# Attention and routed convolution on one core: memory tokens by a factor, the lower part of x formed earlier, lower filters last

## The reference, cut to what matters

```
xn  = rmsnorm(gn(x)) * g1                       # gn: 32 groups of 4 channels
q,k,v = w_qkv @ xn                               # 4 heads of 32 channels
k = concat([mem_k, k], tokens); v = concat([mem_v, v], tokens)   # 4 memory tokens
q = softmax(q, channels of a head) * DHEAD**-0.5
k = softmax(k, tokens)                           # over the 4 + 1024 tokens
context = k @ v.T ;  out = context.T @ q         # per head
x = x + rmsnorm(w_out @ out + b_out) * g2
# second block: 3x3 convolution whose filters are a sum of 3 experts, weighted
# per image and input channel by gates from a small routing network on pooled gn(x)
x = x + conv(gn(x), sum_k r[k] * expert[k])
```

## Time and profile before

| what | value |
|---|---|
| median of 3 runs | 440.47 us (439.46 to 441.87) |
| span of the profiled execution | 438.3 us |
| PE busy | 414.9 us, 95% |
| VectorE busy | 351.1 us, 80% |
| ScalarE busy | 296.2 us, 68% |
| GpSimd busy | 265.0 us, 60% |
| granted TensorE clock | 90% or more of full speed in each of 40 slices |

### The profile page before, as it was taken

The page is one execution under the profiler, slowest core; times in us unless marked ns, Lnnn a source line. Parts: engine busy times, 40 slices in busy tenths (PEclk is TensorE's granted clock), DMA queues, the critical chain, the costliest instruction groups (busy, mean ns, idle before and its releaser), DMA issues.

```text
span 438.3 us, 8984 instructions
## 1 busy us (share of the span) xinstructions
PE 414.9 (95%) x2651; PEld 367.2 (84%) x2651; DVE 351.1 (80%) x769; ACT 296.2 (68%) x908; POOL 265.0 (60%) x249
## 2 busy tenths in 40 slices
PE   7789898999999999999999999999999999999987
PEld 6688787979898988889797988888898989778777
DVE  3565989797989889797989798898989696987540
ACT  2785857868676858778676868688686868654131
POOL 4754739567583939486674939385874748252330
PEclk9999999999999999999999999999999999999999
DMA  7420242216252442506262433516162523424331
GB/s 195 178 98 2 96 193 98 120 72 241 99 218 119 146 192 95 229 28 228 98 241 96 175 160 126 208 53 230 52 239 96 192 97 114 175 98 191 146 143 48
DMA packets 19075, 61.63 MB, mean 141 GB/s; under 512 B 3024, under 2 KB 4320, under 8 KB 19040
## 3 DMA queue, kind: packets, MB, share of 16 engines
q1 hardware_dynamic: 19040, 61.21, 37.0%
HBM read 19.29 MB, written 8.39 MB: 63 GB/s over the span
## 4 chain that ended last, share of the span: by engine, by line
PE 43%; DVE 22%; issue 17%; ACT 11%; DMA 2%; POOL 1%; DVEq 0%; SPq 0%; ACTq 0%; POOLq 0%
PE ps_conv L1282 13%; PE ps_y L1214 6%; PE ps_att L1181 5%; DVE w_full L1020 5%; ACT expert_raw L662 4%; DVE y_scaled L908 3%; DVE route_terms L974 3%; ACT qk L601 3%; PE ps_y L1204 3%; PE ps_y L1220 3%; DVE q_exp L860 2%; DMA xa<-in_x_dram 2%; ACT squares L574 2%; PE ps_qkv L1160 2%; PE ps_qkv L1162 2%
## 5 line engine op out<-in xcount | busy, mean ns | idle before, releaser
L601 ACT ACTIVATE qk<-ps_qkv,scale 128x256 f32<-128x256 f32 x128 | 55.7, 471 | 5.9 <-PE ps_qkv L1162 3.5
L544 POOL TENSOR_TENSOR left_hi<-zeros 128x32 fp32r<-128x32 f32 x16 | 9.4, 585 | 78.9 <-DMA right_lo<-img_lo 78.9
L668 ACT ACTIVATE w_hi<-w_full 128x1152 fp32r<-128x1152 f32 x16 | 18.7, 1168 | 52.9 <-DVE w_full L1026 52.9
L537 POOL TENSOR_TENSOR w_lo<-w_full,w_hi 128x1152 fp32r<-128x1152 f32 x16 | 42.8, 2675 | 11.0 <-ACT w_hi L668 6.1
L492 POOL TENSOR_TENSOR x_lo<-x,x_hi 128x1024 fp32r<-128x1024 f32 x16 | 38.4, 2399 | 13.1 <-ACT x_hi L591 13.1
L518 POOL TENSOR_TENSOR scale<-ssq,minus_half 128x8 f32<-128x8 f32 x16 | 26.2, 1639 | 32.9 <-DVE ssq L901 32.9
L642 ACT ACTIVATE y_scaled<-ps_y 128x128 f32<-128x128 f32 x128 | 33.5, 294 | 14.5 <-PE ps_y L1214 14.5
L1160 PE MATMUL ps_qkv<-wqk_hi,x_hi 128*128 128x256 f32 x128 | 40.6, 317 | 2.5 <-ACT x_nt L582 1.3
L1282 PE MATMUL ps_conv<-left_lo,w_hi 128*128 128x512 f32 (+2 forms) x96 | 40.6, 424 | 0.0
L1282 PE MATMUL ps_conv<-img_hi,w_hi 128*128 128x512 f32 (+1 forms) x96 | 36.4, 393 | 2.5 <-issue 1.4
L1282 PE MATMUL ps_conv<-right_hi,w_hi 128*128 128x512 f32 (+2 forms) x96 | 37.9, 395 | 0.0
(11 more groups left out here) (172 smaller groups left out, 1337.5 us busy)
## 6 DMA issues: line engine op xcount, KB each, us to landing
xa<-in_x_dram SPq DMA_DIRECT2D x16, 512.0 KB, 4.1
xb<-in_x_dram SPq DMA_DIRECT2D x16, 512.0 KB, 4.7
left_hi<-img_hi SPq DMA_DIRECT2D x16, 511.5 KB, 2.9
right_hi<-img_hi SPq DMA_DIRECT2D x16, 511.5 KB, 3.7
left_lo<-img_lo SPq DMA_DIRECT2D x16, 511.5 KB, 2.9
right_lo<-img_lo SPq DMA_DIRECT2D x16, 511.5 KB, 3.7
out_dram<-expert_raw SPq DMA_DIRECT2D x15, 512.0 KB, 2.9
expert_raw<-_conv_expert_weight_dram SPq DMA_DIRECT2D x1, 1728.0 KB, 9.0
```

Of the source, the lines that this page charges most:

```text
L537: nc.gpsimd.tensor_tensor(w_lo[p][:, :, :].rearrange("p t o -> p (t o)"), w_full[:, :], w_hi[p][:, :, :].bitcast(F32).rearrange("p t o -> ...
L601: nc.scalar.activation(qk[:, t, :], ps_qkv[t % 2][:, 0:QK], ACT.Copy, scale=scale1[:, t:t + 1]).then_inc(qkv_done, 1)
```

## The change

- Memory tokens: their share of the softmax differs from one image to the next only by one factor per channel, exp(memk_max - k_max_all). Their exponents, their product with the values and with w_out are formed once (`memory_weights`, `memory_keys`, `memory_context`, `memory_mix`). Per image ACT forms `mem_factor` and the denominator `k_den`, VectorE `mem_scale` and `mix_base`, and `mix_evacuate` adds `mix_base` in place of the bias. The two PE products with the memory tokens and the small subtraction and exponent are gone.
- `k_shift` is a transpose in place of a product.
- `high1` on ACT stands before the results and the upper filters; `low1` on POOL stands before `image_edges`, and `x_scale` behind `normalise1`.
- In a convolution the products with the lower filters come last, so that only these wait for w_lo.
- `spreads` has two operations for both columns, a square and a sum, in place of one operation for each column.
- `gn2_mean` is on ACT; two convolution products stand before `y_transpose` in place of after it.

```diff
@@ POOL
             def step(t, p):
                 do(rms1, t, p, 3)
                 do(routing_products, t, p, 5)
-                do(x_scale, t, p, 3)
                 turn(inverse_deviations, t, p, 2)
                 do(gn1_shift, t, p, 2)
                 do(normalise1, t, p, 2)
+                do(x_scale, t, p, 3)
                 do(rms2, t, p, 4)
+                do(low1, t, p, 2)
                 do(image_edges, t, p, 5)
                 do(filters_low, t, p, 5)
-                do(low1, t, p, 2)
                 do(q_normalise, t, p, 3)
@@ ACT
+            def memory_factor(b, p):
+                nc.scalar.activation(mem_factor[:, :], k_max_all[:, :], ACT.Exp, bias=memk_max[:, :], scale=-1.0).then_inc(mem_factor_done, 1)
+            def k_denominator(b, p):
+                nc.scalar.activation(k_den[:, :], mem_sum[:, :], ACT.Identity, bias=k_x[:, C:C + 1], scale=mem_factor[:, :]).then_inc(k_den_done, 1)
...
                 do(qkv_evacuate, t, p, 2, 7)
+                do(high1, t, p, 1)
                 do(results, t, p, 5, 0)
                 do(filters_high, t, p, 4)
                 do(q_exponent, t, p, 2)
-                do(high1, t, p, 1)
                 do(squares1, t, p, 1, 0)
-                do(memk_exponent, t, p, 2)
+                do(memory_factor, t, p, 2)
                 do(k_exponent, t, p, 2)
...
                 do(k_x_evacuate, t, p, 2)
+                do(k_denominator, t, p, 2)
@@ DVE
             def k_subtract(b, p):
-                v.tensor_tensor(memk_exp[0:MEM, :], memk_t[:, :], ps_att[0:MEM, 0:HID], ALU.subtract).then_inc(memk_sub_done, 1)
...
-                for i in range(c.start, c.stop):
-                    last = v.scalar_tensor_tensor(spread[:, i:i + 1], dev[:, i:i + 1], dev[:, i:i + 1], meanvar[:, i, 1:2], ALU.mult, ALU.add)
+                v.tensor_tensor(dev_sq[:, c], dev[:, c], dev[:, c], ALU.mult).then_inc(dev_sq_done, 1)
...
+                v.tensor_tensor(spread[:, c], dev_sq[:, c], meanvar[:, c, 1], ALU.add).then_inc(spread_done, 1)
+                v.tensor_tensor(mem_scale[:, :], mem_factor[:, :], k_rsum[:, :], ALU.mult).then_inc(mem_scale_done, 1)
+                v.scalar_tensor_tensor(mix_base[:, :], mem_mix[:, :], mem_scale[:, :], bias_share[:, :], ALU.mult, ALU.add).then_inc(mix_base_done, 1)
...
                 do(context_mask, t, p, 2)
+                do(mix_start, t, p, 2)
                 turn(variances, t, p, 0)
                 do(mix_evacuate, t, p, 2)
-                do(gn2_mean, t, p, 4)
@@ PE
-                mm(ps_att[:, 0:HID], k_max_all[:, :].to_broadcast((128, 128)), ident[:, :], start=True, stop=True).then_inc(k_shift_ps, 1)
+                tr(ps_att[:, 0:HID], k_max_all[:, :].to_broadcast((128, 128)), ident[:, :]).then_inc(k_shift_ps, 1)
-                mm(ps_att[:, 0:CEXT], memk_exp[:, :], mem_ones[:, :], start=True, stop=False)
-                mm(ps_att[:, 0:HID], memv_t[:, :], memk_exp[:, :], start=True, stop=False)
-                    products = [(n, part) for n in range(TAPS) for part in range(3)]
-                    pe.wait_ge(w_lo_done, b + 1)
+                    products = [(n, part) for n in range(TAPS) for part in range(2)] + [(n, 2) for n in range(TAPS)]
+                conv(2)
                 do(y_transpose, t, p, 2)
-                conv(3)
+                conv(1)
```

More of the change, by code:

```diff
@@ L93, in attention_condconv_kernel @@
         memk_max = sb("memk_max", [128, 1])
+        memk_rel = sb("memk_rel", [128, MEM])
+        memk_weight = sb("memk_weight", [128, MEM])
+        mem_sum = sb("mem_sum", [128, 1])
         memk_t = sb("memk_t", [MEM, HID])
-        memv_t = sb("memv_t", [128, HID])
-        mem_ones = sb("mem_ones", [128, CEXT])
+        memv_t = sb("memv_t", [MEM, HID])
+        mem_context = sb("mem_context", [128, HID])
+        mem_mix = sb("mem_mix", [128, C])
         expert_raw = sb("expert_raw", [128, K, C * TAPS])
@@ L131, in attention_condconv_kernel @@
         k_exp = sb("k_exp", [128, NT, HID])
-        memk_exp = sb("memk_exp", [128, HID])
+        mem_factor = sb("mem_factor", [128, 1])
+        k_den = sb("k_den", [128, 1])
+        mem_scale = sb("mem_scale", [128, 1])
+        mix_base = sb("mix_base", [128, C])
         q_max = sb("q_max", [128, NT * HEADS])
@@ L649, in image_high, with gn2_mean @@
                 nc.scalar.activation(img_hi[p][:, :, :], image(x2[p][:, :]), ACT.Identity, bias=nmean[(p + GAP) % 2][:, 1:2]).then_inc(img_hi_done, 1)
+            def gn2_mean(b, p):
+                act.wait_ge(nmean_done, b + GAP + 1)
+                if past(b, 2):
+                    act.wait_ge(result_done, 2 * (b - 1))
+                nc.scalar.activation(gmean2[p][:, :], nmean[(p + GAP) % 2][:, 1:2], ACT.Copy, scale=-1.0).then_inc(gmean2_done, 1)
             def gate_exponent(b, p):
@@ L725, in step @@
                 do(image_high, t, p, 3)
+                do(gn2_mean, t, p, 3)
                 do(qkv_evacuate, t, p, 1, 2)
@@ L1067, in step @@
                 do(gn1_aggregate, t, p, -1)
+                once(memory_mix, t, 1)
                 do(filters_second, t, p, 3)
@@ L1172, in k_shift @@
                 pe.wait_ge(k_max_all_done, b + 1)
-                mm(ps_att[:, 0:HID], k_max_all[:, :].to_broadcast((128, 128)), ident[:, :], start=True, stop=True).then_inc(k_shift_ps, 1)
+                tr(ps_att[:, 0:HID], k_max_all[:, :].to_broadcast((128, 128)), ident[:, :]).then_inc(k_shift_ps, 1)
             def key_contexts(b, p):
-                pe.wait_ge(memk_exp_done, b + 1)
                 pe.wait_ge(k_exp_done, b + 1)
                 pe.wait_ge(x_scaled_done, b + 1)
-                mm(ps_att[:, 0:CEXT], memk_exp[:, :], mem_ones[:, :], start=True, stop=False)
                 for t in range(NT):
-                    last = mm(ps_att[:, 0:CEXT], k_exp[:, t, :], x_nt[p][:, t, :], start=False, stop=(t == NT - 1))
+                    last = mm(ps_att[:, 0:CEXT], k_exp[:, t, :], x_nt[p][:, t, :], start=(t == 0), stop=(t == NT - 1))
                 last.then_inc(k_x_ps, 1)
@@ L1271, in convolution @@
                             pe.wait_ge(img_lo_done, b + 1)
-                        if by_pass and n == 0 and part == 2 and h == 0:
+                        if n == 0 and part == 2 and h == 0:
                             pe.wait_ge(w_lo_done, b + 1)
@@ L1315, in step @@
                 do(project, t, p, 1, 1)
+                once(memory_keys, t, 1)
                 conv(1)
@@ L1330, in step @@
                 conv(4)
+                once(memory_context, t, 1)
                 do(project, t, p, 1, 4)
```

97 lines of the change are left out of this document (71 added, 26 removed).

## The result

The changed kernel takes 474.36 us (median of 4 runs, 472.08 to 477.04) against 440.74 us for the one before (439.46 to 441.87): 1.0757 times as long, 95% interval 1.0718 to 1.0796. The prediction was 460, from 437 to 474. The sign and the two holds that it named are right, the size is not: +33.6 in place of +19.5, and the median lies just outside the range. The profiled execution has a span of 475.3 us, 37.0 more than before. It is the slowest of the four (477.04 us), with a mean granted clock of 0.953; the other three were granted 0.967 to 0.978.

The account below looks back on a forecast made before the run. Bound: a ring where PE and VectorE wait for each other in turn. Per interval -0.57 - 0.15 + 1.1 + 1.3, taken as +1.65, times 11: +18.2; fill +3, tail -2: 460 us, own range 451 to 469, over cases 437 to 474.

Parts of the forecast that it names:

- The sign: Whole kernel: slower, chance 0.77; faster by more than 2.2 us 0.18, within that 0.05.
- the two holds: Second half of a step: GpSimd's x_scale makes route_terms stand 1.1 us, its x_lo makes k_quarter stand 1.3 us.
- The ring and its two halves: PE and VectorE wait in turn: y_transpose to route_y 11.93 us, route_y to the end of y_scaled 12.06 us.
- First half -0.57: y_transpose to route_y: PE's path 0.9 shorter, VectorE's 0.57; the lesser gain, 0.57 us a step, was taken.
- x_scale holds the first route_terms, 1.1: Head of the second half: x_scale behind x runs from 11.0 to 12.9, so route_terms stands 1.1 us (0 to 1.6).
- low1 holds k_quarter, 1.3: Second half: x_lo starts after w_full, runs until 310.4, and k_quarter stands 1.3 us (0 to 2.3).
- the third rival: Second half: x_lo gets ahead of w_full, 2.3 in place of 1.3 on some 13 steps; 473 us, chance 0.08.
- every tenth added to VectorE is added to the step: Second half: each 0.1 us more on VectorE lengthens the step by 0.1 us, since PE stands idle at its end.
- The fill +3 (0 to 5): Fill steps ahead of the middle: the same two holds against k_half and k_quarter, +3 us, between 0 and 5.
- The tail -2: Two last intervals and last image: no x_scale beside route_terms, partly no x_lo, less waiting for w_lo; -2 us (0 to -3).
- The odd steps -0.15: Steps with an extra stall: ssq no longer meets q_normalise, half of 0.3 us goes, -0.15 an interval.
- The first rival, 429 without holds: No GpSimd hold on VectorE: 13 intervals shorter by 0.57 + 0.15, fill and tail by 1 to 3; 429 us, chance 0.17.

Follow-up runs that it names:

- both moves back: The change with x_scale and low1 both back at their old places on GpSimd, every other edit kept: 444.21 us.
- experiment 4: The change with x_scale and low1 back, memk_rel behind gn1_aggregate of step 0: 442.70 us; with high1 back behind q_exponent too: 440.64 us.

## Why the prediction was wrong in size, point by point

- **The ring and its two halves**: right. The time moved with the two halves and, new, the gap between them.
- **First half -0.57**: right within 0.15, -0.69. It is no sum of its parts: with both moves back it is -0.41, and pairs of spreads alone bring 0.16.
- **x_scale holds the first route_terms, 1.1**: the place is right, the size is 0.65, since gvar and with it x came sooner than taken: x_nt ran from 327.72, 10.6 behind `y_transpose`, and not from 11.0. Besides, a hold is some 0.15 less than what is left of GpSimd's operation, against "as long as" in the prediction: its own row at 154.84 has a hold of 0.16 with 0.33 left. Undone, it gives 6.5 us beside an early x_lo, and only 0.6 where x_lo is back, in a comparison in which the fill gives 4.6 the other way.
- **low1 holds k_quarter, 1.3**: here the forecast took the wrong branch. "w_full has the better of it by a tenth" was a margin that the estimates of the times around it could not carry; x_lo leads in 10 of 13 steps, and the hold is 2.15. This was the third rival, given a chance of 0.08. Its 473 us lies near the measured 474 by luck: it has the 2.3 of w_full in each of 13 steps, but x_scale at 1.1 and nothing for the clock. On the mean the hold by x_lo makes +1.8 in the second half. With the smaller hold of x_scale it happens to sum to +2.45, where I had 1.1 + 1.3 = 2.4; the two errors cancel.
- **"In the second half every tenth added to VectorE is added to the step, since PE stands idle at its end already"**: this is the step that failed. It takes the idle time of PE as free. In 8 of 12 intervals PE was granted half its clock for 3.4 us at and behind its wait, and the products there then ended later than VectorE. That term, +0.79 an interval and 9 us over eleven, stood nowhere in the sum; the products that fill PE's wait give it back in the interval, and the kernel with them, 468.5 us, is inside the forecast's own 451 to 469. Without the term the middle would have been +19.4, against the 18.2 forecast for eleven intervals. The other three runs of the change have no trace; by their higher clock the term should be smaller there.
- **The fill +3 (0 to 5)**: +6.5 to the second `y_transpose`, outside its bounds. k_half (1.88 once) and k_quarter (1.47 and 2.12) are held as forecast; the hold of memk_rel in the setup, which I had not looked for, and stretches with a lower clock come on top. How the 6.5 divide among them is not shown.
- **The tail -2**: -1.0 by this count, which begins at the fourteenth start. The forecast's begins at the thirteenth, and by it the tail is +2.2 and the eleven intervals ahead of it +28.3: I had let a full middle interval (27.3 in place of 24.1, from 371.74) pass as one without holds.
- **The odd steps -0.15**: near. ssq, 0.27 on the mean of eleven middle steps before (up to 0.79), takes 0.15 in each of them after, which is 0.12 and part of the -0.69 of the first half; with both moves back it takes 0.36, and the first half gains only 0.41.
- **The first rival, 429 without holds**: with all holds of the change undone the kernel takes 440.6, so this rival was too fast by 11.6 us. Its first half gained 0.47, but route_y then came 0.5 sooner while x, behind x_nt on GpSimd, stayed where it was (medians 11.02 behind `y_transpose`, 11.08 before), and the first route_terms is held by it for 0.2 more; the fill takes the rest. What holds the fill's last 2 us is open.

## What to carry to other kernels

Ask of every long GpSimd operation that is moved what VectorE does beside it, and where two start within some tenths of a microsecond, price both orders with like chances: the profile of before cannot tell which one leads, and here the two are 2.1 us a step apart. A stall that makes TensorE idle can have a second price, the lower clock behind it; look whether something short stands behind the wait on which the other engine depends. And count what an edit does to a hold only on the path that ends last: mix_base, held by 0.3 us, gained nothing by being formed earlier, and moved behind gvar it was held by 1.7 and cost 1.1 us a step (25.15 for 24.09).

## What the hardware showed that I had not expected

- A VectorE operation on 128x4 elements with one tensor in SBUF (memk_rel) took 2.14 us beside x_lo, and 0.70 at its later place in experiment 4; w_full, with two inputs of 128x1152, is held by 2.15. The size of what is held is no measure.
- GpSimd's small powers held nobody: 15 of the 16 img_lo began within one, and all 16 took 1.28 or 1.29. In the step shown, scale2 (`ssq` to the power of -0.5, 128x8) ran from 330.97 for 1.64 us, and img_lo, with two inputs in SBUF, took its usual 1.29, all but the last 0.36 of it within scale2. scale2 reads SBUF too, so here the exclusion for the whole instruction that the section named above states does not show, and the measurement decides:

```profile
330.97 1.64 POOL L525 TENSOR_TENSOR scale<-ssq,minus_half 128x8 f32<-128x8 f32 x1 [1.35 <-DVE ssq L970]
```

```profile
331.68 1.29 DVE L1025 SCALAR_TENSOR_TENSOR img_lo<-x,nmean,img_hi 128x1024 fp32r<-128x1024 f32 x1
```

- GpSimd is held the same way: x_lo takes 3.61 behind w_full (2.40 by itself), and left_hi, 0.24 by itself, 1.36.
